# One-hot rows of the token lists: eight comparisons with one value per partition each, in place of one broadcast comparison per part

## The reference

```python
x = x + tanh(g_xattn) * attention(layernorm(x), ctx, ctx, ...)
xt = layernorm(x).reshape(3584, 256)
S = sigmoid(xt @ Wg).T                      # 8 experts x 3584 tokens
G, I = top_k(S, 896)                        # each expert picks 896 tokens
hid = gelu(einsum('ekh,ehf->ekf', xt[I], W1) + b1)
out = (einsum('ekf,efh->ekh', hid, W2) + b2) * G[..., None]
x = x + tanh(g_ffn) * zeros.at[I].add(out)
```

## Time and profile before

| | |
|---|---|
| median of the runs | 1002.07 us |
| the profiled execution, its own time | 1000.14 us |
| its span, first to last instruction | 998.4 us |
| mean granted TensorE clock | 0.949 |
| TensorE matmul busy | 871.5 us (87%) |
| VectorE busy | 684.4 us (69%) |
| ScalarE busy | 608.0 us (61%) |
| GpSimd busy | 233.4 us (23%) |

### The profile page before, as it was taken

One profiled execution on the slowest core, in us unless ns is written; L12 is line 12 of the kernel. 1 busy time (PEld: TensorE's weight loads), 2 busy tenths in 40 slices (PEclk: granted clock), 3 DMA queues, 4 the chain that ended last, 5 costly groups with the idle time before them and its releaser, 6 DMA issues. The chain is left out here.

```text
span 998.4 us, 23233 instructions
## 1 busy us (share of the span) xinstructions
PE 871.5 (87%) x8875; PEld 697.9 (70%) x8875; DVE 684.4 (69%) x1875; ACT 608.0 (61%) x1300; POOL 233.4 (23%) x197
## 2 busy tenths in 40 slices
PE   6888999999999999999998501199999999999995
PEld 3546777677767777676766300189999999999995
DVE  7786778777787787777887487674756657574440
ACT  2756777777777777777766310084856748467471
POOL 4740000000000000000000040324656656555313
PEclk9999999999999999999999755599999999999998
DMA  8826465465564654746631120415253451525203
GB/s 192 196 41 144 113 145 140 112 167 121 132 150 114 156 134 119 167 116 138 140 80 30 29 84 0 134 37 122 47 123 68 114 135 47 130 53 147 31 8 37
DMA packets 96211, 104.65 MB, mean 105 GB/s; under 512 B 11744, under 2 KB 92272, under 8 KB 96112
## 3 DMA queue, kind: packets, MB, share of 16 engines
q1 hardware_dynamic: 84128, 88.50, 35.6%
q0 software_dynamic: 10752, 14.69, 8.7%
q10 hardware_dynamic: 1232, 0.12, 0.1%
HBM read 39.60 MB, written 14.68 MB: 54 GB/s over the span
## 5 line engine op out<-in xcount | busy, mean ns | idle before, releaser
L419 DVE TENSOR_REDUCE a_nm<-a_pS 112x1 f32<-112x375 f32 x512 | 264.7, 543 | 95.0 <-PE a_pS L620 91.7
L285 ACT ACTIVATE a_P<-a_pT 128x448 f32<-128x448 f32 x384 | 209.0, 546 | 138.6 <-PE a_pT L614 137.9
L620 PE MATMUL a_pS<-a_kst,a_qst 96*112 96x375 bf16 x512 | 151.5, 335 | 3.1 <-DVE a_nm L419 2.7
L614 PE MATMUL a_pT<-a_qst,a_kst 98*128 98x112 bf16 x1536 | 139.4, 213 | 2.6 <-DMA a_qst<-a_mT 2.6
L614 PEld LDWEIGHTS a_pT<-a_qst,a_kst 98*128 98x128 bf16 x1536 | 107.5, 99 | 43.6 <-issue 11.6
L1375 PE MATMUL e_p<-w2h,e_hh 128*128 128x256 f32 x448 | 128.4, 287 | 0.0
L1375 PE MATMUL e_p<-w2h,e_hl 128*128 128x256 f32 x448 | 126.3, 282 | 0.0
L1375 PE MATMUL e_p<-w2l,e_hh 128*128 128x256 f32 x448 | 126.3, 282 | 0.0
L976 POOL MEMSET r_factors<- 128x1 f32 x15 | 0.6, 101 | 510.3 <-POOLq L62 510.1
L1230 POOL DMA_INDIRECT out_dram<-e_y,e_idx x56 | 88.4, 1578 | 133.5 <-ACT e_y L1259 130.0
L1300 DVE TENSOR_TENSOR e_hl<-e_hid,e_hh 128x384 fp32r<-128x384 f32 (+1 forms) x128 | 77.6, 623 | 52.0 <-ACT e_hh L1254 51.5
(11 more groups left out here) (202 smaller groups left out, 1557.5 us busy)
## 6 DMA issues: line engine op xcount, KB each, us to landing
a_kst<-a_kp SPq DMA_DIRECT2D x192, 192.0 KB, 3.7
w<-in_L_ffn_W_dram SPq DMA_DIRECT2D x16, 1024.0 KB
a_qst<-a_qp SPq DMA_DIRECT2D x96, 112.0 KB, 3.7
a_craw<-in_ctx_dram SPq DMA_DIRECT2D x32, 128.0 KB
a_xin<-in_x_dram SPq DMA_DIRECT2D x8, 448.0 KB, 6.6
a_xb<-in_x_dram SPq DMA_DIRECT2D x32, 112.0 KB, 3.0
out_dram<-a_x SPq DMA_DIRECT2D x32, 112.0 KB, 2.3
xn_scratch<-a_x SPq DMA_DIRECT2D x32, 112.0 KB, 2.5
```

The source lines that it names most:

```text
L285: act.activation(P[quad % 2][:, c, :], pT[u % 2][:, 0:4 * LQ], ACT.Exp).then_inc(exp_done, 1)
L419: dve.tensor_reduce(nm[:, h:h + 1], pS[h % 2][0:LQ, 0:LK], AXX, ALU.max, negate=True).then_inc(s_used, 1)
L614: last = pe.matmul(pT[u % 2][:, j * LQ:(j + 1) * LQ], kst[b % 4][:, h, c * 128:(c + 1) * 128], q_of(b, slice(None), h), start=True, stop=True)
L620: pe.matmul(pS[h % 2][0:LQ, 0:LK], q_of(b, slice(0, ROWS), h), kst[b % 4][0:ROWS, h, 0:LK], start=True, stop=True).then_inc(s_ready, 1)
```

## The change

The tile `iota_l` (0 to 127 in each partition) becomes bf16, and `list_rows` makes each batch's 128 columns with an instruction of its own, which compares `iota_l` with one f32 value per partition, the token's `lo`. The semaphore is raised by the last of the eight. One call of `list_rows` issued one instruction of 1024 columns before, and issues eight of 128 after.

```diff
-    T.iota_l = sb("iota_l", [LQ, 128])
+    T.iota_l = sb("iota_l", [LQ, 128], BF16)
...
     n = B // 4
     wait(dve, T.l_used, at(4, j - 3))
-    dve.tensor_tensor(T.L[j][:], T.iota_l[:].unsqueeze(1).to_broadcast([LQ, n, 128]),
-                      T.place_e[:, 1, j * n:(j + 1) * n].unsqueeze(2).to_broadcast([LQ, n, 128]), ALU.is_equal)\
-       .then_inc(T.l_ready, 1)
+    for b in range(n):
+        last = dve.tensor_scalar(T.L[j][:, b, :], T.iota_l[:], T.place_e[:, 1, j * n + b:j * n + b + 1], None, ALU.is_equal)
+    last.then_inc(T.l_ready, 1)
```

## The result

The changed kernel takes 1004.53 us (median of 18 runs, 1002.78 to 1006.67); the kernel before, on the same chip, 1002.12 (18 runs, 1001.02 to 1004.44). The ratio is 1.0022, 95% interval 1.0015 to 1.0029: slower by 2.2 us. The profiled execution has a span of 1003.7 us, 5.3 more than before.

| stretch | before | after | difference |
|---|---|---|---|
| to the first product of expert 0's list | 628.49 | 630.09 | +1.60 |
| from there to the first product (L1363) of expert 0 | 23.28 | 23.78 | +0.50 |
| length of that first product, first to last start | 20.43 | 20.87 | +0.44 |
| first products of experts 1 to 4 | 4 x 19.40 | 20.35, 20.23, 19.59, 20.21 | +2.78 |
| all the rest | | | 0.0 |

What follows compares the result with a forecast made beforehand. TensorE was taken to bound the kernel from 647.83 us on, expert 0's gathers and VectorE's routing before that. List +0.6 and gathers -0.7 gave -0.1 on an expected median of 1002.07: forecast 1002.0 us, range 999.6 to 1004.8.

Steps and rivals of the forecast that it cites:

- The list of expert 0: In routing, where VectorE sets the pace alone: 32 short comparisons at 0.16 us replace four broadcasts, +0.57 us.
- The rows' reading of the operand's price: In each short comparison on VectorE, the one value per partition costs 0.065 us of its 0.16.
- The cheap and the dear rivals: Each short comparison costs 0.10 us (cheap: 999.8 us, chance 0.12) or 0.20 us (dear: 1003.2 us, chance 0.10).
- The gathers of expert 0: Beside expert 1's list, GpSimd's gathers lose 0.8 us to VectorE instead of 1.91, so GpSimd finishes 1.1 us sooner.
- starved rival: Expert 0's gathers get their turn only after the whole series of short comparisons: 1005.7 us, slower, chance 0.18.
- the term of -0.7 us: Before expert 0's first product: the part of the gathers' gain that reaches the kernel, at most 0.9 us.
- at 364 GB/s they end at 646.2: Transfers for expert 0's gathers and the next weights, 2.99 MB after 638 us, end at 646.2 us, not about 647.1.
- The six other lists: Lists of experts 2 to 7, in the expert steps: 0.6 us longer each, hidden in VectorE's idle time, so 0.
- TensorE waits for nothing: In the expert steps TensorE has no waits, so longer lists on VectorE there cost no kernel time.
- what would prove it wrong: TensorE waits in the expert steps, for instance for subtractions held up behind eight slow comparisons.
- The products read the same L, in the same layout: TensorE's list products read the same list parts L, laid out as before; no time was added for them.

Runs made afterwards that it cites:

- after_same: The change in full plus an unused tile of 256 bytes a partition, so later tiles stand where they stood in the kernel before: 1001.24 us, ratio 1.0001.
- early_all: The change in full, with the expert steps' four series after subtractions 4, 5, 6 and 14 instead of 5, 8, 11 and 14: ratio 1.0001 to the kernel before.
- late_gathers: As steps, but GpSimd issues the next expert's gathers only after the 14th subtraction of a step: ratio 1.0377 to the kernel before.
- lists01: The kernel before with short comparisons only in the lists of experts 0 and 1, the six step lists keeping the broadcast: ratio 1.0016.
- after_p256: The change in full plus 512 unused bytes a partition, so later tiles stand 256 bytes above their places in the kernel before: ratio 1.0008.
- steps: The kernel before with short comparisons only in the six lists of the expert steps, broadcast in those of experts 0 and 1: ratio 1.0032.
- first_paired: The kernel before with expert 0's list alone made by one all-bf16 comparison per part, batch innermost: 995.18 us, ratio 0.9941.
- paired: All lists made by one all-bf16 comparison per part, batch innermost, TensorE reading every eighth column: ratio 1.0045 to the kernel before.

## Why the prediction was wrong

- **The list of expert 0** was right: 0.1625 us from start to start for 0.16, and +0.66 us for +0.57. The rows' reading of the operand's price held (0.065 us). The Trainium skill's table ("VectorE: DVE Perf Modes", TRN2 errata), whose 94 ns have no term for it, did not: by it the series would take 3.0 us, and it takes 5.2. The cheap and the dear rivals fall with it.
- **The gathers of expert 0**: the price of each was too high (0.2 us forecast, 0.02 measured), so that the starved rival is false and GpSimd gains 1.9 us and not 1.1. (The rule that the prediction weighed, the Trainium skill's "SBUF — State Buffer", the trap where DVE blocks DMA, would have had these series hold the gathers; no gather shows it: over all profiles 124 gathers run beside such comparisons and nothing else on VectorE, and they take 0.94 to 1.05 us.) But none of it arrives, and the term of -0.7 us measured 0. The step that failed is "at 364 GB/s they end at 646.2": after, too, 7 us pass at full rate (367 GB/s) and the last 3 us at 143. The tail is not made by GpSimd's pace. What makes it, no run tells.
- **The six other lists**: this is the step that failed and turned the result. "TensorE waits for nothing" held for the kernel before, and the sum priced the edit by VectorE's idle time alone. In the changed kernel TensorE has 2.8 us of waits there in the profiled execution. The prediction had named such waits as what would prove it wrong, but blamed subtractions held up behind the series. They were done in time (the one that ScalarE needed at 715.74 had ended at 712.68); what was late is TensorE's signal to ScalarE, by up to 1.63 us. The term of the six lists, which the sum put at 0, measured +2.8 us.
- **"The products read the same L, in the same layout"**: true of the layout, not of the place. The smaller iota moved every later tile by 256 bytes. Put back (after_same), the change costs 1.0001 (0.9992 to 1.0010), which holds both nothing and the 0.66 us of the list. So the measured loss is that of the short comparisons at these addresses, in this order: with the first three series moved forward (early_all) it is gone at the same addresses.

With +0.66 and 0 for the gathers the sum without the waits is 1002.7 us, and the 1.8 us up to the measured median are of the size of the waits.

What stays open. Two conditions are shown to be needed for the waits: the place of the tiles (after against after_same, in the times of all runs as in the profiles) and gathers in the second half of the first product (late_gathers). That short comparisons in the steps are needed too rests on one profiled execution of lists01 and is not shown by its times; late signals come without them. What the signals contend with is not shown, nor the rule of the addresses: after_p256 and steps have the same one and differ fivefold, each in one execution. lists01 measures 1.6 us over before, of which its profile shows 0.7. A broadcast comparison on undisturbed gathers was not tried, since the one disturbs the other.

**Which version to take.** first_paired is 6 us faster than before. By the two runs against before, 0.9941 with the paired list and 0.9954 with the same tiles unused, some 4.6 us of that are the place of the tiles and 1.3 the list. The intervals of the two overlap, so the times don't show the second part; the profiles have 1.97 us for it. For the first, 64 bytes are enough.

## What to carry to other kernels

An edit that changes the size of a tile moves every tile declared behind it, and here 64 bytes were worth more (0.4%) than the edit that was to be judged (0.2%, and nothing that could be measured at the old addresses): compare with a spare tile that keeps the addresses, and try a shift as an edit of its own. Price a producer's pace by who waits for its data: GpSimd's 1.9 us were real and bought nothing, since the transfers were no sooner done. One profiled execution can be the luckiest of its kernel, as that of lists01 was: see where it stands among the runs before its lack of waits is taken for the kernel's. An engine with slack can still have a part in stopping the engine that sets the pace; look in the profile after for waits between engines that the edit didn't touch.

## What the hardware showed unexpectedly

- The second product's matmuls (128x256, fp32r) stand 120.0 ns apart with e_hh at address 148800 of a partition and 116.8 with it at 148864 or 150912, the weights unmoved. Only the latter two are multiples of 128; all others, 148544 to 157248, are 64 bytes past one. That is not the whole rule: paired's 149184 is too, and has 118.3. All later tiles move together, so which of them matters is not shown.
- A signal from TensorE to ScalarE came 1.63 us after the end of the matmul that raised it (714.08 to 715.71). In a kernel with the same schedule to 0.1 us (after_same) ScalarE took up the same piece without a wait. Such signals were late in ten of the twelve kernels whose tiles stood at -256, +256, +384 or +512 bytes, and in none of the eight at 0, +64, +2048 or +2112.
- Series of 128-column bf16 comparisons with one value per partition left a gather at 0.94 to 1.05 us; beside the two-source broadcasts alone, 1.14 us apart, it took 1.86 and 1.95. Two-source f32 subtractions stretch it too: to 1.71 us in each step of the change, and with a broadcast beside them to 2.95 in the kernel before.
- A bf16 comparison of two sources with neighbouring elements takes 0.60 us for 1024 columns, against 1.14 with an f32 source and broadcasts; and the 32 list products take 1.98 us with every eighth column loaded, against 0.81 with neighbouring ones, both at the full granted clock.
